# State-space layer of an eight-layer kernel: which steps' product with B is made on GpSimd

## The reference

```python
x = x + _L1_attn_b_ref(_layernorm(x, axis=-1), L1_attn_b_W_up, ..., L1_attn_b_b_down)
```

```
h[t] = exp(delta[t, d] * A[d, s]) * h[t-1] + (delta[t, d] * xs[t, d]) * B[t, s]
y[t, d] = sum over s of h[t] * C[t, s]   + skip[d] * xs[t, d]
```

## Time and profile before

| | |
|---|---|
| median of 3 runs | 1880.45 us (1879.37 to 1882.93) |
| the profiled execution | 1880.12 us |
| its span, first to last instruction | 1877.9 us |
| mean granted clock of TensorE | 0.967 |
| busy over the whole span | TensorE 92%, VectorE 74%, GpSimd 51%, ScalarE 48% |
| the state-space layer in the span | about 1241 to 1697 us |

### The profile page before, as it was taken

How to read it: one execution, slowest core, us unless ns; L and a number is a source line. 1 busy time by engine, 2 the same in 40 slices (tenths; PEclk the granted TensorE clock), 3 DMA queues, 4 the chain that set the end, 5 groups by cost and what they waited for, 6 DMA issues and landing times. The chain is left out here.

```text
span 1877.9 us, 23760 instructions
## 1 busy us (share of the span) xinstructions
PE 1719.7 (92%) x7374; PEld 936.2 (50%) x7381; DVE 1387.3 (74%) x2189; ACT 906.7 (48%) x2131; POOL 950.4 (51%) x986
## 2 busy tenths in 40 slices
PE   6889988999999899979998999988898988889999
PEld 2346654555555466646665566533243333335665
DVE  5868876555555488856776677579999999997765
ACT  3335544545555355536555433556455464443332
POOL 3833332434333233432121255478989989785555
PEclk9989999999999899979998999989999999899999
DMA  6001110000000011110000133210000000002333
GB/s 246 1 17 52 52 51 12 1 1 1 1 1 1 13 46 48 55 68 1 1 2 1 63 98 103 86 34 1 17 1 13 5 6 12 1 2 81 101 97 108
DMA packets 39995, 70.37 MB, mean 37 GB/s; under 512 B 6400, under 2 KB 13696, under 8 KB 39104
## 3 DMA queue, kind: packets, MB, share of 16 engines
q1 hardware_dynamic: 39872, 68.87, 11.4%
HBM read 64.00 MB, written 1.70 MB: 35 GB/s over the span
## 5 line engine op out<-in xcount | busy, mean ns | idle before, releaser
L2138 POOL TENSOR_TENSOR ssm_hc<-ssm_h,ssm_cm 128x512 f32<-128x512 f32 x256 | 324.2, 1288 | 43.1 <-DVE ssm_h L2192 41.4
L307 PE MATMUL banks<-ffn_x_high,up_high 128*128 128x512 f32 x544 | 291.0, 535 | 8.6 <-DVE ffn_hg L920 3.9
L2077 PE MATMUL banks<-ssm_hc,const 128*128 128x512 f32 x512 | 267.4, 604 | 0.2
L2192 DVE TENSOR_TENSOR_SCAN ssm_h<-banks,ssm_dbx 128x512 f32<-128x512 f32 x208 | 249.7, 1217 | 5.8 <-issue 3.5
L2122 ACT ACTIVATE banks<-banks,a_neg 128x510 f32<-128x510 f32 x256 | 167.1, 659 | 169.3 <-PE banks L2053 167.6
L1804 POOL TENSOR_TENSOR ffn_a<-ffn_p,ffn_wide 128x512 f32<-128x512 f32 x128 | 166.3, 1301 | 142.6 <-PE banks L1736 118.5
L1527 POOL TENSOR_SCALAR wide_pin<-wide_pin,wide_rden 128x256 f32<-128x256 f32 x256 | 117.6, 478 | 221.6 <-DVE wide_rden L1545 221.6
L308 PE MATMUL banks<-ffn_x_low,up_high 128*128 128x512 f32 x544 | 216.9, 399 | 0.0
L309 PE MATMUL banks<-ffn_x_high,up_low 128*128 128x512 f32 x544 | 216.7, 398 | 0.0
L1769 ACT ACTIVATE ffn_th<-banks 128x512 f32<-128x512 f32 (+1 forms) x136 | 80.4, 597 | 181.9 <-PE banks L309 157.4
L1825 DVE SCALAR_TENSOR_TENSOR ffn_p<-ffn_th,banks 128x512 f32<-128x512 f32 (+1 forms) x136 | 93.2, 685 | 99.1 <-ACT ffn_th L1769 57.1
(11 more groups left out here) (218 smaller groups left out, 3414.9 us busy)
## 6 DMA issues: line engine op xcount, KB each, us to landing
ffn_wide<-r_kept SPq DMA_DIRECT2D x256, 128.0 KB, 2.9
ffn_wide<-r_kept SPq DMA_DIRECT2D x64, 256.0 KB, 3.1
ssm_packed<-ssm_parts SPq DMA_DIRECT2D x48, 64.0 KB, 2.0
up_whole<-in_up SPq DMA_DIRECT2D x1, 2304.0 KB, 15.3
weights<-in_weights SPq DMA_DIRECT2D x1, 2048.0 KB, 21.7
up_whole<-in_up SPq DMA_DIRECT2D x1, 2048.0 KB, 8.5
weights<-in_weights SPq DMA_DIRECT2D x1, 1168.0 KB, 23.9
weights<-in_weights SPq DMA_DIRECT2D x1, 1152.0 KB, 8.4
```

Source lines behind the costliest of these rows:

```text
L307: pe.matmul(out, w_high, x_high, start=True, stop=False)
L2077: pe.matmul(k.bank[5][:], k.c("hot")[:, P - row:2 * P - row], hc[:, i % LAG, :], start=False, stop=(i % NP == NP - 1)).then_inc(s["red"], 1)
L2138: pool.tensor_tensor(hc[:, i % LAG, :], h[:, i % HOLD, :], cm[:, i // NP % 2, :], ALU.mult) \
L2192: dve.tensor_tensor_scan(h[:, n % HOLD, :], k.bank[DELTA[n % AHEAD]][:], product, 0.0, ALU.mult, ALU.add).then_inc(s["h"], 1)
```

## The change

One line chooses the pooled steps. Before: each step whose number within its pass leaves 4 when divided by 5 (4, 9, ..., 59; 12 in a pass). After: each step whose number leaves 3 when divided by 4, except step 3 of the first pass (7, 11, ..., 255; 15 in the first pass, 16 in the others). The lists `pooled` and `steps`, which number the pooled steps for the waits, follow from it.

```diff
     AHEAD, HOLD, LAG = 3, 4, 6
     DELTA, DELTA_X = (0, 1, 4), (2, 3, 6)
     ALL = PASSES * NP
-    by_pool = lambda i: i % NP % 5 == 4
+    by_pool = lambda i: i % 4 == 3 and i > 4
     pooled = [0]
     for i in range(ALL):
         pooled.append(pooled[-1] + by_pool(i))
```

## The result

The changed kernel takes 1886.33 us (median of 16 runs, 1882.33 to 1888.11), the kernel before 1879.48 (16 runs, 1875.42 to 1883.01) beside it. The ratio is 1.0032, 95% interval 1.0024 to 1.0040: slower by about 6 us, where 3.4 us of gain were forecast and 1881.0 was the upper end of the range.

A forecast was written before the change was run, and what follows sets the result against it. VectorE was taken as the bound, GpSimd close behind and TensorE from `gated` to step 24. 8.7 - 1.2 - 2.25 - 1.1 - 0.75 = 3.4 us gain gave 1877.0 us, range 1873.0 to 1881.0.

The forecast's parts named there:

- The gain of 8.7 us: VectorE loses 15 products of 0.58 us; the most that can come back, if VectorE bounds everywhere.
- (a), the start: First pass up to step 24: nothing to save, since both rules pool five steps there.
- (a), `gated` to step 24: Passes 2 and 3: TensorE's chain sets the time, so one saved product a pass is worth nothing; 1.2 us off the gain.
- (b), the burst: Step 24 to `gated`: four GpSimd `rest` at slots 46 to 53 delay scans 58 and 59; 0.75 us a pass, 2.25 in all.
- (d), collisions: VectorE's `dx` at slot 41 waits beside `pdbx` 43, about 0.5 us a pass; half of 1.5 taken, 0.75 us lost.
- (c), the last pass: Four more steps pooled after its step 9 save 2.3 us; half taken off, 1.1 us, with bounds 0 and 2.3.
- What follows the layer: A chain on TensorE behind the layer, said to start that much sooner and hide nothing.
- The rival on the slower side: GpSimd's products in the steady cycle reach 1.274 us or more instead of 1.23; +9 us, 1889; chance 0.07.
- The second rival: GpSimd becomes the bound and eats all the gain, the burst costing 1.9 us a pass; time 1880.4; chance 0.22.

The follow-up runs named there:

- the kernel with 23 for 24: The kernel before, with step 23 pooled in place of step 24 in the last pass only; 1882.59 us (one run) beside 1880.22.

## Why the prediction was wrong

The sign was wrong. Step by step, with what each was given and what it measured as after against before (minus is a gain):

**The gain of 8.7 us** was there as work: 15 products of 0.58, with `dbx` and `pdbx` at the durations taken. VectorE is busy for 434.40 us of the layer in place of 436.07, so even of its own busy time all but 1.7 us came back. Most of these 7.0 us are collisions: 2.6 at `fix` and `dx`, and in the last pass VectorE is busy for 3.7 us more than four saved products would leave.

**(a), the start: given 0, measured +1.84.** The working said that the first pass has no such step to save because both rules pool five up to step 24, and left it there. It compared counts and not places. That the first pooled step moved from 4 to 7 costs 1.2 us of it, shown by pooling step 4 alone; GpSimd's products cost none of it, since the kernel without them has it too.

**(a), `gated` to step 24: given 0, measured +1.66 in pass 2 and nothing in pass 3.** That the saved product is worth nothing there was right: pass 3 shows it. What was missing is the clock, which I took as given there. With matmuls ahead of the close it stayed whole and the 1.7 us were gone; whether by TensorE's work or by another phase, that kernel alone doesn't say. Another phase can do it: the clock is whole there with step 4 pooled, and with the copy behind the exponential.

**(b), the burst: right.** The hole of scan 58 was to grow from 0.5 to 1.3 and grew to 1.33; over the three passes that is 2.16 us where 2.25 were given (in pass 2 it was 0.84 before).

**(d), collisions: given 0.25 us a pass, measured 0.87.** The mechanism and the place were right (`pdbx` runs when `dx` is issued), the size was half of the upper bound; `dx` took a little more than the whole bound, +0.58, and a second instruction, `fix`, came to it with +0.28. With 1.74 saved, 0.83 lost at scan 58 and 0.87 here, the stretch from step 24 to `gated` should gain 0.04; it gained 0.07 in passes 1 and 3 and 0.19 in pass 2. So of the 1 us that it was forecast to fall (its own terms, with (d), give 0.74), collisions took nearly all.

**(c), the last pass: given a gain of 1.2 (2.3 less 1.1), measured +3.1.** This is the largest miss, 4.3 of the 9.6 us between forecast and result. Its bounds, a loss of 0 to 2.3 off the saved products, had no room for a pass that gets longer. Its 3.9 us of holes were also read too low: the 110.70 us end 2.66 us before the last `gated`, for which VectorE waits. I knew by the earlier trace rows that VectorE and GpSimd hinder each other when VectorE has two SBUF inputs, and applied it to `dx`; the eighth layer's pieces on VectorE, of the same kind, I didn't look up. By the landmarks, `r_top` comes 3.0 us later, `r_score` 3.6 and `r_equal` 4.6; behind it 1.5 are won back. Of the 3.0, 2.44 are the longer `x_low`. That the loss lies ahead of step 40 is shown by the kernel that leaves that stretch alone and gains 1.44; that it isn't GpSimd's load alone, by the kernel with 23 for 24, which loses 2.4 us with as many products as before. For `x_low` itself, one GpSimd product less gave 1.22 us back. That the routing instructions cost the rest is read from their lengths; none of them was moved by itself.

**What follows the layer: given as hiding nothing, measured +1.4.** It meets collisions of its own: before, one of the eighth layer's routing instructions takes 1.20 us where 0.29 is usual (`r_rank`, L443), after it is two others. The kernel without `pdbx` has the same two at the same length, and the kernel with the new rule in the last pass alone has the one of before (179.1 us behind the layer). So it isn't GpSimd's products of the layer that lengthen them; what does is not explained:

```profile
1773.55 1.47 DVE L442 TENSOR_TENSOR_SCAN r_rank<-const,r_equal 128x128 f32<-128x128 f32 x1
...
1775.70 1.42 DVE L445 TENSOR_TENSOR r_over<-r_over,r_equal 128x128 f32<-128x128 f32 x1
```

The step that failed most is (c), and under it one judgement: a collision was priced at what the engine that comes second loses in the earlier trace rows, 0.4 to 0.5 us, and only where I saw one; `x_low` alone lost 2.44. In sum, from -3.4: start +1.8, clock +1.7, burst and collisions in the passes 1 to 3 +1.9, last pass +4.3, which makes +6.3; the layer measured +6.24.

The rival on the slower side had the right sign by the wrong mechanism. It needed GpSimd's products at 1.274 us or more from start to start in the steady part. There VectorE's cycle of four steps, from pooled scan to pooled scan (1286.02 to 1292.27), is 6.25 us, as forecast. The second rival (GpSimd eats all) comes near in number for the passes 2 and 3 without the clock, 112.25 and 112.31 against 112.55 and 112.42, but not by its mechanism: it had the burst cost 1.9 us a pass, and the burst cost 0.84 at most, the collisions 0.87.

The Trainium skill (SBUF — State Buffer, Who interferes with whom) has the pair of instructions right: scans and `dbx` beside `pdbx` stayed at 1.21 and 0.67 us, `dx`, `fix`, `x_low` and the routing got longer. The prediction left out its exception, that copies, casts and tensor-scalar instructions can take the shared pair in a two-port mode with one input; the cast `r_mask` at 1.29 us for 0.21 fits it. That the later one waits is half of it here: `x_low` waited for three GpSimd instructions in a row, and for two when one was taken away. Its advice against offloading between these two engines (Perfetto Trace Analysis, Optimizing Scalar/DVE Operations) came out true for this change, with 17.1 us between the kernel with the 63 products and the one without; for the 3 products of the middle, where each pass gained 0.5 us, it did not.

**What stays open.** What picks the close at which the clock falls; how step 4 brings the clock back sooner; why two routing instructions behind the layer are long in some kernels and one in others; and by what rule VectorE is let in between two GpSimd instructions once (`x_low` at 1.08) and not another time (3.52). Each was reproduced or switched, none explained.

## What to carry to other kernels

When work is moved to GpSimd, list first every VectorE instruction with two SBUF inputs in the stretch, and the casts and tensor-scalar ones, also those of the next layer, and price each at up to the whole run of GpSimd instructions that may stand beside it. In the last pass here a slot that kept off them was worth more than one product more. Compare two rules by which steps they pick and not by how many. Between engines this close to each other, a gain of half a microsecond in one part can be a change of phase for all that follows, so a gain found alone has to be measured again in the sum.

## What the runs showed of the hardware

A VectorE instruction with two SBUF inputs took 3.52 us where 1.08 is its usual time, beside three back-to-back GpSimd instructions of unchanged length, and 2.30 with one of them gone. A cast with one SBUF input took 1.29 us beside a GpSimd product, and 0.21 in the kernel before. VectorE's scans and products with one operand in a bank stayed at 1.21 and 0.67 us beside a GpSimd that was busy for 106 of 112 us.

The granted clock of TensorE fell to half (1.2 GHz) for 3 to 4 us at one close of a pass, and cost 1.6 to 1.8 us there. It fell at the same place in both profiles of a kernel (two each of two kernels), and at another place after an edit that lies more than 45 us ahead of it.
